# Rebuilding the attention stage of a transformer block: unrolled, tiles in pairs, one part of four heads at a time

## What is computed

```
x = x + layernorm(attention(layernorm(x)))      # 16 heads of 128, 4 key heads, rotary q and k, causal softmax, Wo
x = x + layernorm(moe(layernorm(x)))            # top 6 of 64 experts, and a shared expert
```

## Time and profile before

| | before |
|---|---|
| median of 3 runs | 2516.22 us (2512.63 to 2517.93) |
| span of the profiled execution | 2515.8 us |
| first scores start | 167.94 us |
| last `output` of PE starts | 1998.80 us |
| PE busy, whole span | 2040.1 us (81%) |
| DVE, ACT, POOL busy | 1578.2, 1186.3, 715.7 us |

### The profile page before, as it was taken

The page is one execution under the profiler, slowest core; times in us unless marked ns, Lnnn a source line. Parts: engine busy times, 40 slices in busy tenths (PEclk is TensorE's granted clock), DMA queues, the critical chain, the costliest instruction groups (busy, mean ns, idle before and its releaser), DMA issues. The chain is left out here.

```text
span 2515.8 us, 46912 instructions
## 1 busy us (share of the span) xinstructions
PE 2040.1 (81%) x15459; PEld 1825.9 (73%) x15459; DVE 1578.2 (63%) x3449; ACT 1186.3 (47%) x2906; POOL 715.7 (28%) x760
## 2 busy tenths in 40 slices
PE   1269999999989999998999999899999747636630
PEld 1159999989879998887899989789998625434420
DVE  5237676766877766688676767876676548810008
ACT  2026566656556666555566656556666411111110
POOL 0012332323323333223333323333333100034542
PEclk9969999999999999999999999999999957756655
DMA  9600101020110001011100020110100022145535
GB/s 371 261 17 26 43 2 43 2 76 18 43 52 26 18 27 40 38 43 51 44 15 29 1 77 18 43 51 26 43 1 1 1 91 74 42 142 130 132 98 183
DMA packets 71749, 153.57 MB, mean 61 GB/s; under 512 B 9496, under 2 KB 52392, under 8 KB 67928
## 3 DMA queue, kind: packets, MB, share of 16 engines
q1 hardware_dynamic: 62840, 126.60, 14.6%
q0 software_dynamic: 8672, 24.02, 3.5%
HBM read 106.34 MB, written 44.26 MB: 60 GB/s over the span
## 5 line engine op out<-in xcount | busy, mean ns | idle before, releaser
L387 PE MATMUL s_ps<-kT,qT 128*128 128x512 f32 (+3 forms) x2304 | 577.0, 367 | 23.3 <-PE prod_ps L353 9.2
L568 ACT ACTIVATE pT<-t_ps 128x512 fp32r<-128x512 f32 (+3 forms) x768 | 349.3, 491 | 390.6 <-PE t_ps L396 387.4
L408 PE MATMUL av_ps<-pT,v 128*128 128x256 f32 (+1 forms) x3840 | 502.3, 283 | 19.8 <-ACT y_part L584 17.0
L408 PEld LDWEIGHTS av_ps<-pT,v 128*128 128x128 f32 x3840 | 472.7, 191 | 34.8 <-issue 18.7
L493 DVE TENSOR_REDUCE neg_max<-s_ps 128x1 f32<-128x128 f32 (+7 forms) x512 | 385.5, 753 | 126.0 <-PE s_ps L387 117.8
L387 PEld LDWEIGHTS s_ps<-kT,qT 128*128 128x128 f32 x2304 | 406.7, 194 | 66.2 <-issue 31.9
L560 ACT ACTIVATE probs<-s_ps,neg_max 128x128 f32<-128x128 f32 (+7 forms) x512 | 381.7, 746 | 120.8 <-DVE neg_max L493 119.5
L500 DVE TENSOR_TENSOR pT<-t_ps,pT 128x512 fp32r<-128x512 f32 (+3 forms) x768 | 400.9, 549 | 25.9 <-ACT pT L568 19.5
L616 POOL TENSOR_TENSOR roped<-rope_c,rope_s 128x256 f32<-128x256 f32 (+1 forms) x192 | 124.2, 647 | 972.6 <-DVE rope_s L483 666.7
L629 POOL TENSOR_TENSOR y<-y,y_part 128x512 f32<-128x512 f32 x224 | 287.9, 1285 | 306.3 <-ACT y_part L584 306.3
L396 PE MATMUL t_ps<-ident,probs 128*128 128x128 f32 x2304 | 342.0, 275 | 7.3 <-DVE pT L500 7.3
(11 more groups left out here) (166 smaller groups left out, 2144.6 us busy)
## 6 DMA issues: line engine op xcount, KB each, us to landing
w_a<-w_split SPq DMA_DIRECT2D x16, 1024.0 KB, 5.4
w_o<-w_split SPq DMA_DIRECT2D x16, 1024.0 KB, 6.6
e_w_in<-in_expert_w SPq DMA_DIRECT2D x8, 1536.0 KB, 7.8
w_split<-w_hl SPq DMA_DIRECT2D x4, 2560.0 KB, 15.3
xT_split<-pre_xT SPq DMA_DIRECT2D x4, 2048.0 KB, 9.7
xT<-xT_split SPq DMA_DIRECT2D x4, 2048.0 KB, 7.9
w_b<-w_split SPq DMA_DIRECT2D x16, 512.0 KB, 4.2
f_m<-sums SPq DMA_DIRECT2D x8, 1024.0 KB, 11.4
```

Source lines behind the costliest of these rows:

```text
L387: last = pe.matmul(out, qT[:, h // 2, a, h % 2, rows], kT[:, group % 2, s, lo:hi], start=(n == 0), stop=(n == 2))
L408: last = pe.matmul(av_ps[:, cols], v[:, group % 2, a, j], pT[:, n % 2, s, j, cols], start=(j == 0 and m == 0), stop=(j == 2 * p + 1 and m ...
L568: act.activation(pT[:, (k // 2) % 2, 0, first:first + count, (k % 2) * P:(k % 2 + 1) * P], t_ps[n % 2][:, 0:count * P].rearrange("p (j n) ...
```

## The change

`prepare` goes; one `attention` program, wholly unrolled, does all. Rows go in **macros** of 8: the four heads of a big tile (7-m), then the four heads of a small tile (m), for m = 0 to 3; 4 macros a group, 64 in all. e = s % 8 is the place in a macro. A **part** is one tile's four heads; its attend is over 512 columns at once.

What each engine does in step s, in this order:

- PE: `scores(s+1)`; the side units of step s; `transpose_probs(s-1)`. `after_transposes` is empty.
- DVE: `inverse(s)`, `row_max(s+1)`, `probs_low(s-1)`, its part of the side units of step s, a norm stage.
- ACT: `probs_high(s-1)`, `exponentials(s+1)`, its part of the side units of step s, `rope_high` of step s-2.
- POOL: `scale(s)` (probabilities times the inverse row sum, in place), `rope_low` of step s-3, `rope_add` of step s-1, weight splits, norm stages.

q, k and v units, x transposes and outputs share one bank, `misc_ps`; `begin_misc` waits until its last user has been read. q and k are made with the head dimension on partitions: no transposes; rotation is DVE times cos, ACT copying the bank's two halves of partitions over each other, POOL times sin and add. Output sums four heads in PSUM (12 matmuls), and DVE adds the sum to `y`.

```diff
+def before_transposes(s):
+    macro, e = divmod(s, 8)
+    g, m = divmod(macro, MACROS_PER_GROUP)
+    ...
+    if e == 1 and macro >= 1:
+        out.append(("av", 2 * macro - 1, 2))
+    if e in (2, 4) and macro + 1 < MACROS:
+        out.append(("q", macro + 1, e // 2 - 1))
+    if e == 1 and there and g % KV_HEADS == 2 and b + 1 < B:
+        out.append(("xt", b + 1, m))
+    if e in (0, 3) and macro >= 1:
+        out.append(("out", 2 * macro - 2 + e // 3, 0))
+    if e in (5, 7) and there:
+        out.append(("av", 2 * macro, (e - 5) // 2))
+    if e == 6 and g + 1 < GROUPS:
+        out.append(("k" if m < 2 else "v", g + 1, m % 2))
+# PE
+            def begin_misc(unit):
+                if not MISC_AT[unit]:
+                    pe.wait_ge(table_read, 4)
+                    return
+                kind, of, n = MISC_ORDER[MISC_AT[unit] - 1]
+                if kind == "xt":
+                    pe.wait_ge(xt_lo, 4 * of + n + 1)
+                elif kind in "qk":
+                    pe.wait_ge(swap_done, ROPE_AT[kind, of, n] + 1)
+                elif kind == "v":
+                    pe.wait_ge(v_lo, V_AT[kind, of, n] + 1)
+                else:
+                    pe.wait_ge(y_done, of + 1)
+            def transpose_probs(r):
+                pe.wait_ge(scaled, r + 1)
+                ...
+            def attend(p, half):
+                ...
+                if begin == 0:
+                    pe.wait_ge(t_lo, CHUNKS_BEFORE[4 * p + 4])
+                    pe.wait_ge(v_lo, V_AT["v", g, 1] + 1)
+                    if p:
+                        pe.wait_ge(av_lo, p)
+                for j in range(begin, end):
+                    for n, (a, s) in enumerate(((0, 0), (0, 1), (1, 0))):
+                        last = pe.matmul(av_ps[:], v[:, g % 2, a, j], pT[:, s, part_slot(p) + j], ...
+            def output(p):
+                g = p // 8
+                begin_misc(("out", p, 0))
+                pe.wait_ge(av_lo, p + 1)
+                pe.wait_ge(o_lo, g + 1)
+                ...
+            for s in range(-1, ROW_STEPS):
+                if s + 1 < ROWS:
+                    scores(s + 1)
+                for u in before_transposes(s):
+                    unit(*u)
+                if 1 <= s <= ROWS:
+                    transpose_probs(s - 1)
+                for u in after_transposes(s):
+                    unit(*u)
+# DVE
+            for s in range(-1, ROW_STEPS):
+                if 0 <= s < ROWS:
+                    inverse(s)
+                if s + 1 < ROWS:
+                    row_max(s + 1)
+                if 1 <= s <= ROWS:
+                    probs_low(s - 1)
+                for u in units_at(s):
+                    unit(*u)
+                norm = norm_at(s)
+                if norm and norm[2] < STAT_STAGES:
+                    norm_stage(*norm)
+# ACT
+            def rope_swap(kind, of, half):
+                n = ROPE_AT[kind, of, half]
+                act.wait_ge(cos_done, n + 1)
+                act.activation(rope_s[0:64, n % 2], misc_ps[64:128], ACT.Copy)
+                act.activation(rope_s[64:128, n % 2], misc_ps[0:64], ACT.Copy).then_inc(swap_done, 1)
+            for s in range(-1, ROW_STEPS):
+                if 1 <= s <= ROWS:
+                    probs_high(s - 1)
+                if s + 1 < ROWS:
+                    exponentials(s + 1)
+                for u in units_at(s):
+                    unit(*u)
+                for u in units_at(s - 2):
+                    if u[0] in "qk":
+                        rope_high(*u)
+# POOL
+            def scale(r):
+                pool.wait_ge(inv_ready, r + 1)
+                at = probs[:, r % 3, 0:(row_tile(r) + 1) * P]
+                pool.tensor_scalar(at, at, inv_sum[:, r % 16:r % 16 + 1], None, ALU.mult).then_inc(scaled, 1)
+                ...
+                pool.tensor_tensor(at, at, table, ALU.mult).then_inc(sin_done, 1)
+                pool.wait_ge(sin_done, n + 1)
+                pool.tensor_tensor(rope_c[:, n % 2], rope_c[:, n % 2], rope_s[:, n % 2], ALU.add).then_inc(rope_done, 1)
```

More of the change, by code:

```diff
@@ L179, in attention, with big_tile, row_tile, row_chunks @@
-def attention(nc, consts, x, w_split, xT_split, x1_rows, rows):
+MACROS_PER_GROUP = NT // 2
+GROUPS = B * KV_HEADS
+MACROS = GROUPS * MACROS_PER_GROUP
+ROWS = MACROS * 2 * GROUP
+PARTS = 2 * MACROS
+ROW_STEPS = ROWS + 4
+BATCH_STEPS = ROWS // B
+PSLOTS = NT + 1
+def big_tile(m):
+    return NT - 1 - m
+def row_tile(r):
+    m = (r // 8) % MACROS_PER_GROUP
+    return big_tile(m) if r % 8 < GROUP else m
+def row_chunks(r):
+    blocks = row_tile(r) + 1
+    return [(first, min(4, blocks - first)) for first in range(0, blocks, 4)]
@@ L182, in attention @@
+V_AT = {u: n for n, u in enumerate([u for u in MISC_ORDER if u[0] == "v"])}
+Y_NORM, X1_NORM, X_NORM = 4, 21, 44
+STAT_STAGES = 9
+def attention(nc, consts, x, wpack, x1_rows, rows, sums):
     with ExitStack() as ctx:
@@ L270, in produced_at @@
-        def produced_at(k):
-            if k < 0 or k % STEPS not in AT:
-                return None
-            when, unit = AT[k % STEPS]
-            return k // STEPS + (when == "next"), unit
-        def program(eng, slot):
-            for k in range(-1, ROT):
-                slot(k, 0, False)
-            with eng.Fori(0, B - 1) as turn:
-                for k in range(ROT, ROT + BODY):
-                    slot(k, turn, False)
-            for k in range(ROT, NORM_END):
-                slot(k, B - 1, True)
@@ L286, in exists, with tiles @@
[L286 to L300 removed]
+        def tiles(a):
+            return a.rearrange("(t p) n -> p t n", p=P)
@@ L651, in slot @@
-            def slot(k, turn, last):
-                now = produced_at(k)
-                if now and made(now[0], last):
-                    rope_add(*now, turn)
-                if k % 2 == 0 and k >= 4 and exists(k - 4, turn, last):
-                    add_output((k - 4) // 2, turn)
-                norm_part(k, turn, last)
-            pool.dma_start(xb[:], x[0].rearrange("(t p) n -> p t n", p=P)).then_inc(x_in, 16)
-            for unit in range(8):
-                rope_add(0, unit, 0)
@@ L667 @@
+            for s in range(ROW_STEPS, B * BATCH_STEPS + X_NORM):
+                norm = norm_at(s)
+                if norm and norm[2] >= STAT_STAGES:
+                    norm_stage(*norm)
+            pool.wait_ge(zeros_out, 16 * (B + 3))
 TRASH = 48
```

991 lines of the change are left out of this document (495 added, 496 removed).

## The result

The changed kernel takes 2889.99 us (median of 4 runs, 2888.9 to 2896.08) against 2515.15 us for the kernel before on the same chip: a ratio of 1.1492 (95% interval 1.1475 to 1.151). It is 375 us slower, 70 us above the forecast of 2820 and inside the range.

The account below looks back on a forecast made before the run. PE bounds attention, busy 96%. First scores 64, plus 64 macros x (26.0 work + 7.8 waits) = 2163, x transposes 24, norms 40, tail 10 + 30 + 489: 2820 us; range 2640 to 2900, chance 0.57.

Parts of the forecast that it names:

- first scores: Preparation before attention: scores start near 64 us, 55 to 80, instead of 168.
- PE's work: Matmul time in attention: 1665 us, or 26.0 for each of 64 macros, against 1744 before.
- place 0: Output of the big tile waits for its attended high and low parts: mean 1.7 us a macro.
- place 3: Output waits for the bank that q filled one step before, until ACT's copies end: mean 2.9 us a macro.
- place 5: First half of the attend waits for DVE's low parts of the row just transposed: mean 1.15 us a macro.
- place 4: q waits for the previous output's bank, which DVE adds after its low parts: mean 1.55 us a macro.
- x transposes: At place 1 they make the following q wait for ACT and DVE: 2 us, 12 times, 24 us.
- Norms: DVE's last norm steps slowed by waiting for POOL: 3.6 us a norm, 40 us, between 0 and 100.
- Rival 1: Gaps at place 3 drop PE's clock to half: 3010 us if each time, 2880 if one in three; chance 0.2.
- Rival 3: POOL's scale bounds big rows, so transposes wait 1 us on each of four: 256 us more, 3075; chance 0.08.
- Rival 2: DVE and ACT reach side units before transposes, hiding the hand-overs, worth all 499 us: 2320 us; chance 0.12.
- The signs: Trace marks: right, e.g. PE busy near 75% in attention; wrong, e.g. PE over 90% or clock below 0.9.

Follow-up runs that it names:

- 1: The changed kernel with DVE and ACT reading a side unit's bank before they evict the same step's transposes; 2810.22 us, ratio 1.1157.
- 2: The changed kernel with all of PE's side work behind the transposes of the former row instead of ahead of them; 2675.76 us, ratio 1.0627.
- 6: The changed kernel with all side work behind the transposes and the probabilities scaled on DVE instead of POOL; 2587.51 us, ratio 1.029.
- 9: The changed kernel with ACT's two copies of each q or k bank cut from 512 to 64 columns; 2813.75 us, ratio 1.1176.
- Kernel 12: The changed kernel with side work behind transposes except the small tile's attend, scale on DVE, next row's max before inverse and scale; 2512.36 us, ratio 0.9996.
- kernel 5: The changed kernel, order kept, with the probabilities scaled on DVE right behind the inverse instead of on POOL; 2960.25 us, ratio 1.1765.
- 3: The changed kernel with the first q unit one place earlier and the x transposes moved from place 1 to 7; 2893.59 us, ratio 1.1495.

## Why the prediction was right, and where its sizes were off

The sum against the profiled execution, in its own terms: first scores at 68 instead of 64; attention 68 to 2361, 2293 us, instead of 2163 + 24 + 40 = 2227; from there 533 instead of 10 + 30 + 489 = 529. That is 4 + 66 + 4 = 74, the 2894.3 - 2820. The 66 are the difference of two misses that lean against each other: PE's work came out 168 us above its term, its idle time 103 below. With the waits as forecast and the work as measured the sum would be 2820 + 168 = 2988, above the range, so that 2890 lies inside it is in part luck.

- **The mechanism holds.** "A bank filled in step s is released late after the end of step s": PE waits at each predicted place, once a macro (62 to 64 times), for the predicted releaser (named by the profile at places 3, 4 and 5, and by the order of time at place 0), and so say the experiments: taking side units first shrinks the waits (1), taking side work behind nearly removes them (2; some 70 us of place 3's come back once the scale is early, in 6), and a shorter link shortens place 3 by its own length (9).
- **The waits, term by term**, measured against predicted, us a macro: place 3 176.6/64 = 2.8 (2.9); place 0 95.4/64 = 1.5 (1.7); place 5 60.9/64 = 0.95 (1.15); place 4 (31.7 + 16.7 + 14.4)/64 = 1.0 (1.55); x transposes 27.2 in all (24). ACT's copies on 64 partitions take 0.59 each, 1.18 together against the 1.09 that I took. Place 4 was overstated by a third. With the gap of place 3 filled its wait is 80/64 = 1.25, so about half of that miss goes with the clock, probably because at half speed PE's own scores cover more (not shown). The other half is open. PE idles 2293 - 1833 = 460 us in attention where waits, x transposes and norms made 499 + 24 + 40 = 563.
- **Norms** show no cost of their own: the Newton products that read two SBUF inputs average 0.23 us, far from twice 0.74, and no wait on them is in PE's list.
- **PE's work** was the term mis-sized: "26.0 for each of 64 macros", 1665, against 1833 busy. The attends are part of it: (2.35 - 0.40)/8 = 0.244 us of spacing against my 0.23, some 24 us. Most of it is the clock. Kernel 12 issues the same 12,915 matmuls, and in its attention PE is busy 1716 us, 117 less, at a clock of 0.98 (over the whole span 1985.3 against 2111.5). The full-speed time that the clock withheld says about the same: (1 - 0.93) x 2293 = 161 us in the change, (1 - 0.98) x 1915 = 38 in kernel 12. As kernel 12 also stops PE less often, 117 is an upper end; some 27 us are open.
- **A reading that was wrong without a price**: that below 256 columns fewer columns save nothing. In the trace of before, attends of 128 columns start 0.087 us apart on average and those of 256 columns 0.126. The old attends are then 454 us, against my 459.
- **Rival 1, the falling clock, came true beside the forecast**, and I gave it 0.2 as a case of its own. I argued that place 3's gap was "shorter than every gap that shows a fall in attention". That was misread: the trace of before has a fall behind a gap of 1.48 us (the clock is third from last in the third line).

```profile
686.61 0.88 PE L408 MATMUL av_ps<-pT,v 128*128 128x256 f32 x6 [1.48 <-ACT y_part L584]
687.32 2.49 PE L353 MATMUL prod_ps<-w_a,xT 128*128 128x256 f32 x12
688.00:691.00 3.00, 3.00 (x13) 2.71 (x13) 2.31 (x6) 1.16 (x3) 0.00 (x0) 0.50 0.00 0
```

Behind another gap of 1.48 us, before 1619.49, the same 12 matmuls take 1.66, so such a gap may or may not cost the clock, and one of 3 us in every macro had to be priced. The fall happened in most macros, not in one of three. Its price was smaller than the rival's 3 us a macro: at most 117/64 = 1.8 by kernel 12, some 63 us in all by the filled gap. The Trainium skill (TensorE: Matmul & The Clock Gate, "HAM oscillation") describes such a loss in each turn of a loop; here the trace agrees that it comes back, with 48 of 55.
- **Rival 3, POOL**: its condition, a scale dearer than a two-input add, came true (2845 ns for 1024 columns, 2.8 ns each; my bound was 2.6 us, from POOL's add in the earlier trace rows); its consequence didn't, as 31.8 us of waits for it show and kernel 5's loss confirms. The side work that stands ahead of the transposes covers it. It decides only with that cover gone: 251.6 us in kernel 2.
- **Rival 2, all hidden**, needed DVE and ACT to take units first. Kernel 1 made that true by hand and still took 2810: the 499 us were never all to be had that way, since evictions are as urgent as banks. My expectations for kernels 1, 2 and 3 (2530, 2380, 2590) took a wait's whole size as its worth. The waits were measured one by one, but each hides the next one behind it.
- **The signs**: first scores at 68 (near 64), PE's share 80% (near 75%), attend spacing 0.24, and 2293/16 = 143 us for 32 rows (135) are those of "right". The sign for rival 1, a clock below 0.9, didn't show, at 0.93, though the clock fell in most macros: it was set too low to tell.

Open: how the clock's 63 to 117 us divide over the places, beyond the count of falls (54 at place 3, 8 at place 2, 6 at place 0, of 70); why place 4 is shorter even at full clock; and how much of the last 83 us that kernel 12 loses in attention is its own order.

## What to carry to other kernels

Unrolling a pipeline and choosing one fixed place for all side work makes every short step a race between PE and the evictions: add up, for each bank, what the evicting engine has to do first, and compare it with PE's next work in microseconds, not in steps. A unit of work in a gap is at once a victim (it waits for its bank) and a cover (for the row's softmax), so moving it away moves the wait; the sum of the waits isn't what one can win. And where a wait of 2 or 3 us comes back in each turn, read the lengths of the matmuls behind it before costing it at the wait alone.

## What the runs showed of the hardware that I had not expected

- Added matmuls can make a kernel faster: 630 in a recurring gap of 2.8 us took 63 us off, with the clock from 0.93 to 0.98.
- POOL's multiplication by one scalar per partition, a single tensor input, takes 1565 ns for 512 columns and 2845 for 1024; its addition of two tensors takes 1285 for 512 and its copy 612.
- An ACT copy of 64 partitions by 512 columns takes 0.59 us, as long as one of 128 partitions by 512 (0.60).
- DVE's one-input scale of 512 columns takes 0.49 us alone and 1.50, three times that, when begun beside a POOL operation.
- The clock can fall behind a single gap of 1.48 us in a stretch that is otherwise dense, and another gap of that length leaves it at full.
